# A four-layer sequence model on one core: another order for layer 0, wider weighing in layer 3, and score maxima turned by VectorE

## The reference

```python
x = _L0_cond_ref(x, ...)   # linear attention, 8 heads, then norm, scale and shift, silu, projection, + x
x = _L1_cond_ref(x, ...)   # norm, reorder by perm, mamba (conv, scan), reorder back, gate, + x
x = _L2_cond_ref(x, ...)   # norm, two state-space scans, gate, + x
x = _L3_cond_ref(x, ...)   # softmax attention, 16 heads of 16, then norm, scale and shift, silu, projection, + x

# layer 0
q = softmax(xn @ Wq + bq, over the 32 of a head); k = softmax(xn @ Wk + bk + mask, over the tokens)
v = (xn @ Wv + bv) * src_mask
att = einsum('bnhd,bnhl->bhdl', k, v); y = einsum('bnhd,bhdl->bnhl', q, att)
x = x + (silu(_ln(y) * (1 + scale) + shift) @ W_out + b_out)
# layer 3
att = softmax(einsum('bnhl,bmhl->bnmh', q, k) + mask, axis=2)
y = einsum('bnmh,bmhl->bnhl', att, v)
```

## Time and profile before

| | |
|---|---|
| median of three runs | 2146.53 us (2145.2 to 2150.4) |
| profiled execution | 2145.81 us, of which 2144.1 us span |
| mean granted TensorE clock | 0.963 |
| PE, DVE, ACT, POOL busy | 93%, 75%, 67%, 48% of the span |

### The profile page before, as it was taken

How to read it: one execution, slowest core, us unless ns; L and a number is a source line. 1 busy time by engine, 2 the same in 40 slices (tenths; PEclk the granted TensorE clock), 3 DMA queues, 4 the chain that set the end, 5 groups by cost and what they waited for, 6 DMA issues and landing times.

```text
span 2144.1 us, 34726 instructions
## 1 busy us (share of the span) xinstructions
PE 1987.4 (93%) x13528; PEld 1401.5 (65%) x13528; DVE 1599.5 (75%) x2075; ACT 1437.8 (67%) x2434; POOL 1030.6 (48%) x586
## 2 busy tenths in 40 slices
PE   6978999899999899899998999899898999997997
PEld 3854899659985899499956996799642223232333
DVE  5454899469984899499957997799678777776721
ACT  3315999289964998599729986988452555654563
POOL 1011599309981699189903994699341011100000
PEclk9989999999999999999999999999997999998998
DMA  4031111111111121011100110111011111111000
GB/s 181 1 127 40 60 56 59 44 40 55 55 40 51 40 60 55 16 46 55 50 2 25 58 57 22 60 55 55 11 36 34 37 28 29 29 27 25 9 21 20
DMA packets 54161, 95.04 MB, mean 44 GB/s; under 512 B 11815, under 2 KB 20167, under 8 KB 52590
## 3 DMA queue, kind: packets, MB, share of 16 engines
q1 hardware_dynamic: 52462, 88.63, 13.7%
q0 software_dynamic: 1536, 4.20, 0.7%
HBM read 73.29 MB, written 6.91 MB: 37 GB/s over the span
## 4 chain that ended last, share of the span: by engine, by line
PE 75%; issue 8%; POOL 6%; DVE 6%; ACT 4%; DMA 1%; SPq 0%; POOLq 0%; DVEq 0%; ACTq 0%
PE PS L728 14%; PE PS L752 12%; PE PS L733 7%; PE PS L248 6%; PE PS L1437 6%; PE PS L257 5%; PE PS L1389 5%; PE PS L1575 5%; POOL A L883 5%; PE PS L759 2%; PE PS L1121 1%; DVE A L1402 1%; PE PS L615 1%; PE PS L1011 1%; DVE A L868 1%
## 5 line engine op out<-in xcount | busy, mean ns | idle before, releaser
L883 POOL TENSOR_TENSOR A<-A 128x1024 f32<-128x1024 f32 x384 | 898.3, 2383 | 339.4 <-ACT small L807 272.1
L815 ACT ACTIVATE A<-A,negA 128x512 f32<-128x512 f32 x768 | 545.1, 712 | 42.8 <-DVE A L868 33.4
L868 DVE TENSOR_TENSOR_SCAN A<-A,PS 128x512 f32<-128x512 f32 x384 | 433.1, 1199 | 52.2 <-PE PS L733 36.0
L868 DVE TENSOR_TENSOR_SCAN A<-A,small,PS 128x512 f32<-128x512 f32 x384 | 455.2, 1258 | 6.1 <-PE PS L728 5.3
L752 PE MATMUL PS<-ident,A 128*128 128x128 f32 x3072 | 401.4, 274 | 16.3 <-POOL A L883 11.3
L1611 ACT ACTIVATE A<-PS 128x1024 f32<-128x1024 f32 x256 | 262.2, 1024 | 221.8 <-PE PS L1575 220.2
L1402 DVE TENSOR_REDUCE A<-PS 128x1 f32<-128x512 f32 x512 | 330.1, 686 | 79.8 <-PE PS L1389 76.5
L728 PE MATMUL PS<-A 128*128 128x128 f32 x3072 | 386.5, 277 | 0.1
L728 PEld LDWEIGHTS PS<-A 128*128 128x128 f32 x3072 | 366.4, 193 | 7.0 <-issue 3.6
L752 PEld LDWEIGHTS PS<-ident,A 128*128 128x128 f32 x3072 | 348.1, 141 | 23.5 <-POOL A L883 13.9
L792 ACT ACTIVATE A<-A,small 128x512 f32<-128x512 f32 x340 | 240.4, 712 | 23.0 <-PE PS L733 22.8
(11 more groups left out here) (197 smaller groups left out, 1976.9 us busy)
## 6 DMA issues: line engine op xcount, KB each, us to landing
A<-scrc SPq DMA_DIRECT2D x192, 256.0 KB, 3.2
A<-A SPq DMA_DIRECT2D x360, 32.0 KB
scr<-A SPq DMA_DIRECT2D x4, 1024.0 KB, 4.6
W<-in_wa SPq DMA_DIRECT2D x2, 1536.0 KB, 9.7
X<-in_x SPq DMA_DIRECT2D x4, 512.0 KB, 5.5
out<-X SPq DMA_DIRECT2D x2, 1024.0 KB, 4.5
W<-in_w SPq DMA_DIRECT2D x1, 1984.0 KB, 8.1
W<-in_wzc SPq DMA_DIRECT2D x1, 1536.0 KB, 11.8
```

Of the source, the lines that this page charges most:

```text
L815: e.activation(A_B[i % 4], r.DT[:, dt, ci * 512:(ci + 1) * 512], ACT.Exp, scale=negA[:, r.n, dt * 16 + s:dt * 16 + s + 1]).then_inc(*decay ...
L868: e.tensor_tensor_scan(h, a, u, init, ALU.mult, ALU.add).then_inc(*scanned.up((q, i)))
L883: e.tensor_tensor(h, h, CB[k % 2].unsqueeze(1).broadcast_to([128, 2, 512]), ALU.mult).then_inc(*weighed.up((q, pair)))
```

## The change

In layer 0:
- v and q come from one matmul of 512 columns (`w0[:, 0:3:2]`) with one bias matmul; VectorE works by single tiles, and its second half runs a pair behind.
- The k.v products of a batch stand ahead of its turning of q.
- `modulations_t` is taken apart. Layer 1's column modulations and the first of three `row_mods_t` stay ahead of the turning of y, the others go behind the projection. VectorE's part goes behind layer 1's norm. The turning and projecting go batch by batch.
- The output bias is no longer a matmul. POOL adds it to X ahead of time (four additions of 128x1024).
- SP stores the halves before the later weights and modulations. POOL gathers the first half before it takes the power of the second.

In layer 3:
- Weighing is done in two pieces of 512 columns. They stand in heads j = 1 and 3, behind the first half of the item's scores and ahead of the head's own scores.
- The maxima are turned by VectorE in 32 x 32 blocks, SBUF to SBUF, from a padded 128 x 32 tile `MN`. Each head is written to DRAM by four transfers. PE's turning and the copy are gone.
- A unit's sums are copied out while head 3 of the next unit's step 0 is worked on, and turned in step 1 behind head 0.
- Batch 0's output norm: statistics in unit 4, two tiles a step in steps 3 to 6, the rest in step 7. POOL does the last multiplication (eight instructions).

```diff
@@ first_t
-                tokens_t(e, w, ("v", i), ... W0v ..., "l0bv", (i, i + 1))
-                tokens_t(e, w, ("q", i), ... W0q ..., "l0bq", (i, i + 1))
+                for j in range(2):
+                    o = take(w, ("qv", i + j))
+                    e.matmul(o, ones3[0:3, :], ROW3[0:3, 0:512], start=True, stop=False)
+                    for k in range(2):
+                        t = e.matmul(o, XN[:, k, (i + j) * 128:(i + j + 1) * 128], w0[:, 0:3:2, k, :], start=False, stop=k == 1)
...
-            modulations_t(e, w)
-            turn_t(e, w, "sn0", ..., range(4), ...)
-            for i in range(0, NT, 2):
-                w.wait_ge(*act.at(("sn0", i // 4, 1)))
-                tokens_t(e, w, ("o0", i), ..., "l0bo", (i, i + 1))
+            w.wait_ge(*transfer("wa1").at(0))
+            column_mods_t(e, w, 1, wada[1])
+            row_mods_t(e, w, 0)
+            for b in range(NB):
+                turn_t(e, w, "sn0", ..., (2 * b, 2 * b + 1), ...)
+                for i in range(b * TB, (b + 1) * TB, 2):
+                    w.wait_ge(*act.at(("sn0", i // 4, 1)))
+                    tokens_t(e, w, ("o0", i), ..., None, (i, i + 1))
+            w.wait_ge(*transfer("wa3").at(0))
+            column_mods_t(e, w, 2, wada[3])
+            w.wait_ge(*transfer("wa2").at(0))
+            row_mods_t(e, w, 1)
+            row_mods_t(e, w, 2)
@@ first_v
-            modulations_v(e, w)
+            column_mods_v(e, w, 1, "l1ba", "l1g", "l1be")
+            row_sum_v(e, w, 0)
+            w.wait_ge(*pool.at("x_bias"))
...
+            modulations_v(e, w)
@@ max_rows_v, replacing max_rows_t and the copy
-            e.tensor_copy(NMS[0:TB, k % 2, :], bank(("maxima", k))[0:TB, 0:128]).then_inc(*dve.up(("maxima", k)))
+            e.transpose(NMS[:, k % 2, :], MN[:, k % 2, :]).then_inc(*dve.up(("maxima", k)))
@@ weigh_t
-                t = e.matmul(PV[32 * j:32 * j + 32, c // 2, c % 2 * 256:c % 2 * 256 + 256], V[...],
-                             PX[mt % 2][j][:, c * 256:(c + 1) * 256], ...
+                t = e.matmul(PV[32 * j:32 * j + 32, c, :], V[...],
+                             PX[mt % 2][j][:, c * 512:(c + 1) * 512], ...
@@ layer3_t
-                    take(w, key, doubles)
                     for c in range(2):
                         ahead_t(e, w, LEAD + 32 * u + 4 * mt + j, (c,))
-                        if c == 1 and last:
-                            weigh_t(e, w, *last, j)
+                        if c == 0:
+                            if last and j % 2:
+                                weigh_t(e, w, *last, j // 2)
+                            take(w, key, doubles)
...
-                    if last and j == 3 and last[1] == TB - 1:
-                        normalise_t(e, w, last[0])
+                    if j == 0 and u and mt == 1:
+                        normalise_t(e, w, u - 1)
@@ layer3_v
+                    if j == 3 and u and mt == 0:
+                        take_upper_v(e, w, u - 1)
+                    if j == 0 and u and mt == 1:
+                        normalise_v(e, w, u - 1)
+                if u == 4 and 3 <= mt < 7:
+                    stats_v(e, ("lny3", 0), lambda i: Yt[:, i, :], (2 * mt - 6, 2 * mt - 5))
+                if u == 4 and mt == 7:
+                    moments_v(e, w, ("lny3", 0), range(TB))
```

More of the change, by code:

```diff
@@ L306, in row_parts_p, with row_mods_t, row_sum_v @@
                 e.tensor_tensor(RP[2] if p else RB, RB, RP[p], ALU.subtract).then_inc(*pool.up("row_parts"))
-        def row_mods_t(e, w):
-            o = take(w, ("rows", 0))
+        def row_mods_t(e, w, n):
+            wt, a, b = ((wada[1], 512, 768), (wada[2], 512, 768), (wada[2], 0, 512))[n]
+            o = take(w, ("rows", n))
             for k in range(4):
[L311 to L318, removed]
-        def row_mods_v(e, w):
[L321 to L329, removed]
+                t = e.matmul(o[0:2, 0:b - a], sc[:, k, :], wt[:, k, a:b], start=k == 0, stop=k == 3)
+            t.then_inc(*pe.up(("rows", n)))
+        def row_sum_v(e, w, n):
+            o, a, b = ((MW, 0, 256), (MW, 768, 1024), (WR, 256, 768))[n]
+            w.wait_ge(*transfer("row_mods").at(0))
+            w.wait_ge(*pe.at(("rows", n)))
+            e.tensor_tensor(o[:, a:b], bank(("rows", n))[0:2, 0:b - a], WR[:, a:b], ALU.add).then_inc(*dve.up())
+            banks.give(("rows", n), dve.now())
+        def row_mods_v(e, w):
+            row_sum_v(e, w, 1)
+            row_sum_v(e, w, 2)
             w.wait_ge(*dve.now())
@@ L457, in first_t @@
                     t.then_inc(*pe.up(("att", b, h)))
+                for c in (2 * b, 2 * b + 1):
+                    for h in range(2):
+                        o = take(w, ("qt", c, h))
+                        for j in range(4):
+                            w.wait_ge(*dve.at(("qn", (4 * c + j) // 2 * 2)))
+                            t = e.transpose(o[:, j * 128:(j + 1) * 128], Q0[:, 4 * c + j, h * 128:(h + 1) * 128], ident[:, :])
+                        t.then_inc(*pe.up(("qt", c, h)))
             for i in range(0, NT, 2):
@@ L482, in first_s @@
             for i in range(0, NT, 2):
-                w.wait_ge(*pe.at(("v", i)))
-                for j in range(2):
-                    e.activation(V0[:, i + j, :], bank(("v", i))[:, j * 256:(j + 1) * 256], ACT.Copy, scale=col("mask", i + j)).then_inc(*act.up())
-                banks.give(("v", i), act.now())
-                w.wait_ge(*dve.at(("qsub", i)))
+                for j in (i, i + 1):
+                    w.wait_ge(*pe.at(("qv", j)))
+                    e.activation(V0[:, j, :], bank(("qv", j))[:, 256:512], ACT.Copy, scale=col("mask", j)).then_inc(*act.up(("v", j)))
+                w.wait_ge(*dve.at(("qsub", i + 1)))
                 q3 = Q0[:, i:i + 2, :].rearrange("p i (g e) -> p (i g) e", e=32)
@@ L986, in layer1_p @@
         def layer1_p(e, w):
-            w.wait_ge(*transfer("idx").at(0))
-            for b in range(NB):
-                w.wait_ge(*transfer(f"store1_{b}").at(0))
-                gather(e, f"gather1_{b}", lambda j: XR[:, b * TB + j, :], scr1[b])
             for b in range(NB):
@@ L1341, in max_rows_sp @@
             w.wait_ge(*pool.at(("maxima", k)))
-            e.dma_start(scr3[k].rearrange("q (n t) -> n q t", t=128), NMP[k % 2][0:TB, :, :]).then_inc(*transfer(f"max_out{k % 2}").up(k))
+            rows = scr3[k].rearrange("p (n q t) -> q n p t", q=4, t=32)
+            for q in range(4):
+                e.dma_start(rows[q], NMP[k % 2][32 * q:32 * q + TB, :, :]).then_inc(*transfer(f"max_out{k % 2}").up(k))
             w.wait_ge(*transfer(f"max_out{k % 2}").at(k))
@@ L1380, in ahead_t @@
         def ahead_t(e, w, i, halves=(0, 1)):
-            if 0 in halves and rows_due(i) is not None:
-                max_rows_t(e, w, rows_due(i))
             if i < len(items):
```

159 lines of the change are left out of this document (85 added, 74 removed).

## The result

The changed kernel takes 2090.3 us (median of four runs, 2090.25 to 2090.79) against 2147.6 for the kernel before in the same comparison (2145.2 to 2150.4): a ratio of 0.9736, 95% interval 0.9722 to 0.9751. The profiled execution has a span of 2089.04 us, 55.0 less than before. Three single executions, two of the kernel before (6729 and 7147 us) and one of a kernel further down (10744 us), are left out of every ratio here as slow ones.

The account below looks back on a forecast made before the run. PE was taken as the bound in layer 0, then waiting 18.05 us for a gather, and as pacing layer 3's steps. Savings of 23.9 + 6 + 11 + 5.7 + 8 + 3 = 57.6 from 2145.8 gave 2089 us, range 2068 to 2110.

Parts of the forecast that it names:

- Term A: Layer 0: PE resumes after the first gather at 142.6 instead of 166.5 us, 23.9 us less.
- B: Layer 3, steps with items: 6.69 us instead of 6.80 a step, 53 steps, 6 us less.
- C: Layer 3, ends of units: 1.0 us instead of 2.8 each, six ends, 11 us less.
- D: Layer 3, batch 0's output norm: 9.9 us gone from one step, statistics and silu give some back, 5.7 less.
- E: Layer 3, steps after the last item: 4.6 us instead of 5.56, over 9 or 10 steps, 8 us less.
- (1): Layer 0, v and q merged: 4.42 us a pair instead of 5.51, eight pairs save 8.8 us.
- (2) to (6): Layer 0: q.att ends at 98.3, half 0 lands at 130.7, gather starts there, PE resumes at 142.6 instead of 166.5.
- I take nothing: Layer 1's start: half 1's later norm and modulations could delay a PSUM bank; margin only 2 us, no loss counted.
- (7): Layer 3 weighing: a 512-column piece takes 1.0 us, PE's own work a step 5.72, the 0.51 exp wait goes.
- (8): Layer 3: bunched item halves make PE wait 0.27 and 0.16 us for VectorE; a step 6.58, with extras 6.69.
- (12), (13): Layer 3: low clock from 1870 to 1985 us partly gone, 3 less; the 40 items ahead give 0, within 3.
- F: Layer 3, stretch at granted clock 0.91 from 1870 to 1985 us: its remaining cost goes, 3 us less.

## Why the prediction was right, point by point

The forecast was 2089 with a range of 2068 to 2110. That the total is right is luck, because two errors nearly cancel: Term A was 7.5 too high (16.4 arrived), and layer 3's terms were 5 too low (33.7 against 38.6). The 38.6 of layer 3 are, from the two lists of exps: 2.3 at its start, 3.5 for B, 17.6 for C, 6.5 for the norm of D and 1.7 at its silu, 5.8 for E, 1.2 behind the last exp and in rounding.

- **(1) v and q merged.** Failed in size: 4.90 a pair instead of 4.42, 4.9 us saved instead of 8.8. The 0.22 and the 1.72 were read from rows in which like follows like. Where PE goes from the bias matmul to the float32 ones and back it loses 0.29 a tile (done once a pair, it is 0.30 less). VectorE did not set the pace: PE has no gap there.
- **(2) to (6).** q.att ends at 101.1 instead of 98.3: the 3.9 of (1), less 1.0 because PE began v and q at 39.0. The modulations took 8.2 instead of 6.7, at a low clock (6.5 when the changed kernel ran again). Steps 4 and 5 held within 0.4 (4.0 for 3.6, 8.7 for 8.7), the landing took 4.7 for 4.9, the eight tiles were 1.5 shorter, and the gather's 11.8 held. PE resumed 20.9 earlier instead of 23.9. When the changed kernel ran again without the low clock over the k.v products it resumed at 142.6, the forecast's time, again by errors that cancel: (1) took 3.9 too long, but PE began 1.0 earlier, the products had no low clock (the forecast carried over one of the kernel before, 1.6 us), and the tiles were 1.5 shorter. POOL's order carries 5.3 of the 20.9, by the run that undid it, if the longer gather there belongs to it.
- **"They move earlier as a block", and "I take nothing" for what could take it back.** This is the step that failed. Of 20.9 us, 1.0 went in layer 1's xm matmuls (14.90 for their run instead of 13.95), and not by the bank that the prediction named: they follow each other without a gap, but the granted clock stays at 0.50 until 5.5 us behind PE's resumption, where it was 3.6 before, and at that clock each takes 0.85 instead of 0.43. In the run with POOL's old order VectorE had done all modulations 11 us ahead, and their run still took 14.43. And 3.5 went ahead of the scan: three `row_mods_t` take three banks where two took two, the ring stands one further, and the small product's bank (L959) becomes the first one of the turning. The run with the ring one earlier shows it: same instructions, 3.1 us back. The prediction goes by the order of instructions and not by the places in the ring.
- **(7) Wide piece.** 1.0 forecast, 0.99 measured, for a wrong reason: width is worth nothing (the piece cut in two, 1.00). The 0.14 comes once for each stretch of weighing, so what counts is how many places the weighing stands at.
- **(8) PE waits for VectorE.** The waits of 0.27 and 0.16 are 0.29 and 0.16; 6.58 bare is 6.62, with the combination 6.83, on average 6.72 for the 6.69 forecast. B is 3.5 for 53 steps, not 6, and belongs to PE's turning, not to the weighing: with the old places a step is 6.69.
- **(9) Ends.** 54.63 for 54.5. Each of the first three gave 1.95 beyond the plain steps, forecast 1.8. There are seven of them, not six: one more gave 1.8, and three gave 3.0, 3.0 and 4.0, where the kernel before had stretches of lower clock: 17.6 for C instead of 11. This is the term of layer 3 that was most off.
- **(10) Unit 5's norm.** 9.9 gone, as forecast (step 42: 16.74 to 6.83). The statistics cost 2.6 for 2.7, the moments 0.8; with the pieces at their old places neither costs anything, so this too is a price of the bunching. The 1.5 at the silu did not come (12.20 and 12.27).
- **(11) Free steps.** 4.67 for 4.6; but only six steps are free of anything else: E is 5.8 for 8. With the old places they are 5.56 again: here the new placement pays, since the piece no longer needs the exp just before, and it pays 0.8 at each end of a unit (0.87 against 1.64).
- **(12), (13).** The clock is at 1.00 from 1640 to 2066; what that gave is inside C and the silu's 1.7, near the 3 of F. The items ahead gave 1.5 (15.4 us earlier at their first half, 16.9 at the first exp), within the 3.
- **The rivals.** The wide piece came at the forecast's price. PE did wait. The low clock in layer 3 did not come; it was layer 0's that moved the time, and there I had not looked for it. The port lock: the combination took 0.17 in 30 of 32 cases and 1.50 and 1.62 in two, both early next to POOL's splitting, the same count as before. The eight multiplications on POOL held up nothing.

The combination and the block turning in the changed kernel (instructions of one line: shortest, median, longest in ns):

```profile
L1426 DVE TENSOR_TENSOR W<-A x32: 166/166/1621, 1575.9 to 2008.3; 128x8 f32<-128x8 f32 x32
```

```profile
L1380 DVE STREAM_TRANSPOSE W<-W x32: 195/201/211, 1578.5 to 2008.5; 128x32 f32<-128x32 f32 x32
```

## What to carry to other kernels

Where PSUM banks come from a ring, an added or removed `take` shifts every later one: look at which bank each late reader holds, not only at the order of instructions. Price a matmul by a row in which its neighbours are of the same kind as in the new code; here each stretch of float32 matmuls between bfloat16 ones cost 0.2 to 0.3 us for going over and back, and a wider instruction gained nothing where two narrow ones could stand together. With few buffers between two engines, spread what one hands to the other evenly: moving the same work about was worth 0.5 us of a 6.7 us step, and delaying the consumer's piece by one head freed it from a wait.

## What the runs showed of the hardware

- From one execution to the next the granted clock over layer 0's first k.v products was 1.00 or 0.69 in the same program, and PE resumed for layer 1 at 142.6 or 145.6; PE had just done 3.5 us of two-column matmuls. Over all kernels with these matmuls in one piece it was 0.50 to 0.69 over the first 5.5 us of these products in six profiles and 1.00 in five. Why it differs stays open: with these matmuls in four parts the profile had the full clock, but so had five of eleven with them in one.
- Four column groups side by side took 0.43 for 256 and 0.86 for 512 columns, plus 0.14 once however they were cut.
- After a wait for DMA, PE ran at a granted clock of 0.50 for 3.6 us in the kernel before and for 5.5 in the changed one: a float32 instruction of 512 columns took 0.85 there and 0.43 behind it.
- A gather of eight indirect transfers took 11.8 us, with the next eight behind it without a pause (kernel before) or not (changed kernel), and 14.4 in the run in which 1536 KB of weights were transferred beside it; that this is the cause is not shown.
- VectorE's turning of 128 x 32 in blocks took 0.20 us, in all 32 cases.
